# Attention steps with transposes first, scores second and weighing last, transposes three and weighing five units behind the scores

## The reference

```
x = x + LN(attention(LN(x)))
x = x + LN(feed_forward(LN(x)))

attention:  q = rms_norm(x wq), k = rms_norm(x wk), v = x wv      # 32 query heads, 8 key heads, 64 wide
            s = q k / 8 + alibi + mask      # token t sees tokens t-256 .. t
            out = softmax(s) v, then out wo
feed_forward: (silu(x gate) * (x up)) down, 1408 wide
```

## Time and profile before

| what | value |
|---|---|
| median of 3 runs | 1284.79 us (1283.95 to 1285.63) |
| the profiled execution | 1284.65 us, of which span 1282.9 us |
| PE busy | 1200.5 us (94%) |
| PEld busy | 1014.4 us (79%) |
| DVE busy | 910.8 us (71%) |
| ACT busy | 750.8 us (59%) |
| POOL busy | 386.0 us (30%) |

### The profile page before, as it was taken

The page is one execution under the profiler, slowest core; times in us unless marked ns, Lnnn a source line. Parts: engine busy times, 40 slices in busy tenths (PEclk is TensorE's granted clock), DMA queues, the critical chain, the costliest instruction groups (busy, mean ns, idle before and its releaser), DMA issues.

```text
span 1282.9 us, 29210 instructions
## 1 busy us (share of the span) xinstructions
PE 1200.5 (94%) x9016; PEld 1014.4 (79%) x9016; DVE 910.8 (71%) x2386; ACT 750.8 (59%) x1629; POOL 386.0 (30%) x460
## 2 busy tenths in 40 slices
PE   5999999997999899999999999999979979999998
PEld 4868778785777788888888898889867768888876
DVE  4597776867999788788888878788854355646364
ACT  3645455554999797777777777777732234232330
POOL 1000000001689675443445435443421100202021
PEclk9999999998999899999999999999989989999999
DMA  4216263455566565454555455454442252111110
GB/s 165 98 74 247 103 242 131 181 197 191 202 252 236 175 198 181 154 176 145 177 166 187 145 174 165 160 169 151 151 153 105 98 186 70 66 34 66 34 66 34
DMA packets 99259, 189.34 MB, mean 148 GB/s; under 512 B 8032, under 2 KB 36832, under 8 KB 99168
## 3 DMA queue, kind: packets, MB, share of 16 engines
q1 hardware_dynamic: 99168, 188.21, 43.1%
HBM read 116.54 MB, written 71.63 MB: 147 GB/s over the span
## 4 chain that ended last, share of the span: by engine, by line
PE 80%; DVE 9%; issue 4%; ACT 3%; DMA 3%; POOL 1%; DVEq 0%; SPq 0%; ACTq 0%; POOLq 0%
PE bank L1248 18%; PE bank L1379 17%; PE bank L1316 15%; PE bank L1270 10%; PE bank L1279 10%; PE bank L1297 2%; PE bank L1295 2%; PE bank L1296 2%; PE bank L1305 2%; DVE inv_rms L988 2%; DMA q_st<-q_scr 1%; DVE pT_lo L1041 1%; DVE oT_lo L1053 1%; DVE raw L967 1%; DMA w_stage<-wqT 1%
## 5 line engine op out<-in xcount | busy, mean ns | idle before, releaser
L826 ACT ACTIVATE p_sb<-u_sb,low 128x384 f32<-128x384 f32 (+2 forms) x512 | 274.4, 536 | 54.2 <-DVE low L1034 47.4
L1034 DVE CUSTOM_DVE_ANT_0 u_sb<-bank,bias 128x384 f32<-128x384 f32 (+2 forms) x512 | 231.3, 452 | 56.5 <-PE bank L1270 36.0
L1041 DVE TENSOR_TENSOR pT_lo<-bank,pT_hi 128x384 f16<-128x384 f32 (+2 forms) x512 | 232.3, 454 | 36.8 <-ACT pT_hi L833 21.4
L1270 PE MATMUL bank<-k_st,q_st 128*128 128x384 f32 (+2 forms) x1024 | 249.0, 325 | 7.3 <-DMA q_st<-q_scr 3.0
L833 ACT ACTIVATE pT_hi<-bank 128x384 f16<-128x384 f32 (+2 forms) x512 | 206.6, 403 | 68.5 <-PE bank L1279 64.8
L1279 PE MATMUL bank<-ident,p_sb 128*128 128x128 f32 x1152 | 219.0, 281 | 21.8 <-DVE pT_lo L1041 15.3
L1270 PEld LDWEIGHTS bank<-k_st,q_st 128*128 128x128 f32 x1024 | 176.5, 192 | 31.8 <-DVE v_out L1008 3.3
L1279 PEld LDWEIGHTS bank<-ident,p_sb 128*128 128x128 f32 x1152 | 137.9, 141 | 60.3 <-ACT p_sb L826 40.7
L583 POOL TENSOR_TENSOR rstd<-var_eps,minus_half 128x1 f32<-128x1 f32 (+1 forms) x31 | 23.4, 753 | 482.7 <-DVE var_eps L929 482.7
L1295 PE MATMUL bank<-v_st,pT_hi 128*128 128x65 f16 x1152 | 158.4, 193 | 0.5 <-DVE pT_lo L1041 0.5
L1296 PE MATMUL bank<-v_st,pT_hi 128*128 128x64 f16 x1152 | 158.7, 194 | 0.0
(11 more groups left out here) (115 smaller groups left out, 2324.2 us busy)
## 6 DMA issues: line engine op xcount, KB each, us to landing
q_scr<-qk SPq DMA_DIRECT2D x64, 512.0 KB, 2.7
q_st<-q_scr SPq DMA_DIRECT2D x32, 1024.0 KB, 7.8
k_st<-k_scr SPq DMA_DIRECT2D x64, 256.0 KB, 3.1
o_scr<-o_out SPq DMA_DIRECT2D x128, 128.0 KB, 2.5
o_in<-o_scr SPq DMA_DIRECT2D x16, 1024.0 KB, 5.1
k_scr<-qk SPq DMA_DIRECT2D x16, 512.0 KB, 3.1
z_in<-z_scr SPq DMA_DIRECT2D x8, 1024.0 KB, 5.9
v_scr<-v_out SPq DMA_DIRECT2D x4, 1040.0 KB, 5.9
```

Of the source, the lines that this page charges most:

```text
L826: nc.scalar.activation(p_sb[:, u % RING, 0:w], u_sb[:, u % RING, 0:w], ACT.Exp, scale=-1.0, bias=low[:, u % RING:u % RING + 1]).then_inc(p ...
L1034: nc.vector.tensor_tensor_reduce(out=u_sb[:, u % RING, 0:w], in0=bank[u % 2][:, 0:w], in1=bias[:, 2 * u // UNITS, u % REP, at:at + w], sca ...
L1041: nc.vector.tensor_tensor(pT_lo[:, u % RING, 0:w], bank[2 + u % 2][:, 0:w], pT_hi[:, u % RING, 0:w], ALU.subtract).then_inc(pT_ready, 1)
L1270: mm = nc.tensor.matmul(bank[u % 2][:, 0:w], q_st[:, s, r, P * i:P * i + P], k_st[:, s, part, P * key:P * key + w], start=(part == 0), sto ...
```

## The change

The order within a step and three lags change; no instruction is added, taken away or altered.

```diff
-LAGS = {"split": 3, "scores": 0, "transpose": 2, "exps": 0, "weigh": 4, "take": 5, "invert_sums": 6}
+LAGS = {"transpose": 3, "scores": 0, "split": 3, "exps": 0, "weigh": 5, "take": 6, "invert_sums": 7}
...
-            def unit_work(n, u):
+            def unit_work(n, u, kinds=("transpose", "scores", "weigh")):
                 for stage, nn, uu in due(n, u):
                     work = {"scores": scores, "transpose": transpose_p, "weigh": weigh_values}.get(stage)
-                    if work:
+                    if stage in kinds:
                         work(nn, uu)
 
             def attend(n, tile=None):
                 for u in range(UNITS):
-                    unit_work(n, u)
+                    unit_work(n, u, ("transpose",))
                     if tile is not None:
                         m, at = divmod(u - START, STEP)
                         if m in range(4) and at == 0:
                             transpose_o(tile, m)
+                    unit_work(n, u, ("scores",))
+                    if tile is not None:
                         m, at = divmod(u - START - 4, STEP)
                         if m in range(4):
...
                             project_o(tile, m, (2 * at, 2 * at + 1), bank[7])
+                    unit_work(n, u, ("weigh",))
```

## The result

The changed kernel takes 1304.66 us (median of 4 runs, 1302.59 to 1305.82) against 1284.82 for the kernel before (4 runs on the same chip): ratio 1.0155, 95% interval 1.0137 to 1.0172. It is slower, as I had forecast, but by 19.8 us and not by 4. The profiled execution took 1302.59 with a span of 1300.8.

The account below looks back on a forecast made before the run. PE was taken to bound projecting passes (1.50 us a step), a VectorE-ScalarE loop passes 0 to 4 (1.05). 13.5 + 5.1 - 4.7 + 0.5 - 10.3 = +4.1 on 1284.65 gave 1288.8, 8 in 10 within 1277 to 1297.

Parts of the forecast that it names:

- the loop: Passes 0 to 4: split, transposes, scores, `add_bias`, split takes 1.13 a step against 1.05; 2.7 a pass, +13.5 over five.
- the late scalings: Passes 0 to 2: rounding, `round_pT`, split and scaling become one chain; +1.5, +2.4 and +1.2, together +5.1.
- the wait for heads: Pass 3: PE's wait of 2.83 for the head loads goes, since slower passes let POOL catch up; -4.7.
- the drain: End of the attention passes: one more lag, +0.5.
- the projecting passes: Passes 5 to 15: PE's new order of neighbours exposes fewer weight loads; 0.94 saved a pass, -10.3 over 11.
- the anchor: Steps 0 to 11 of a projecting pass: step 12 starts at 13.97 against 14.1 before, so 0.1 saved.
- the neighbours in steps 12 to 31: Projecting passes: 0.055 saved a step in 15 of 20 steps, plus 0.09 of weighing moved out; 0.85 a pass.
- order worth nothing: Rival: weights are exposed as much elsewhere in the new order, passes 5 to 15 give 0; 1299, chance 0.05.

Follow-up runs that it names:

- E10: Changed kernel with TensorE's transposes turning among three banks instead of two in passes 0 to 4: 1300.0 us.
- E9: E1 with each head load issued one store of o earlier in SyncE's queue: 1305.0 us.
- E4: Changed kernel with VectorE's late scalings put between `add_bias` and the split: 1299.3 us.
- E12: Changed kernel with E4's and E9's edits and TensorE's old order in passes 0 to 4 and the first 12 steps of the others: 1281.7 us.
- E6: Changed kernel with one more, unread product per step on TensorE in passes 0 to 4: 1300.8 us, one run.
- E7: Changed kernel with GpSimd's late splits in passes 0 to 2 cut to 16 of 512 columns: 1301.1 us, one run.
- E1: Changed kernel with scores back at the head of TensorE's step, changed lags and VectorE order kept: 1309.0 us.
- E2: Changed kernel with all of TensorE's old step order, changed lags and VectorE order kept: 1301.1 us.
- E11: Changed kernel with the edits of E4, E9 and E10 together: 1283.8 us, ratio 1.0003.

## Why the prediction was wrong

**The sum.** I had +4.1 and the span grew by 17.9. Term by term, forecast and measured: the loop 13.5 and 13.0; the late scalings 5.1 and 10.5; the wait for heads -4.7 and -3.7; passes 5 to 14 -9.4 and -2.2; pass 15, the drain and the start -0.4 and +0.3. So two terms failed: the gain of the projecting passes came out 7.2 too small, and the late scalings cost 5.4 more.

**Direction and mechanism.** Slower, and through the loop that I named: right. E10 takes the loop away and E9 the order that makes it. In pass 4 the transposes' wait for `pT_lo` is 2.7 in the changed kernel, nothing in E10 and 0.6 in E9.

**The loop's price, 2.7 a pass.** Right in size: pass 4 grew by 2.6. The hops were off in detail in the two steps shown above. Scores behind transposes take 0.44 instead of 0.35, so scores to `add_bias` is 0.81 for my 0.73; and the split waits for its rounding, 0.61 for 0.47.

**The late scalings, +5.1 in passes 0 to 2.** This term was half of what it should have been. Passes 0 to 2 grew by 18.3, of which three loops are 7.8; 10.5 is left for a term of 5.1. Against loop and scaling as forecast (37.0, 37.9 and 36.7) 4.0 is missing in pass 0, 0.9 in pass 1 and 0.1 in pass 2. The chain itself was right: E4 gives back 5.4, and with the loop gone the scalings' place is worth 12.4 (E9 and E12). What I left out in pass 0 is that a slower loop also changes what runs beside what, and how much TensorE has to do: two scalings fell on GpSimd's splits and took 1.49 for 0.75, and the full clock came back 17.1 after the pass's start instead of 6.8. I took every duration from the kernel before, where the granted clock of passes 0 to 2 was 0.97 and no scaling of pass 0 was doubled. E6 puts the clock at about 2.4 in pass 0, and E7 the contention at 2.9, but some of that is clock too (0.75 to 0.82), each is one execution, and pass 0 varies by 1 to 2 without a cause in the program (E1, E2, E9). So the two don't add, and how they share the 4.0 is not settled.

The two loops are not terms of a sum either. E10 without the loop gives back 6.0 in passes 0 to 2, E4 with a shorter chain 5.4, E11 with both (and earlier loads) 16.5 of 116.6. Each holds the time up when the other is gone.

**The wait for heads in pass 3, -4.7.** Mostly right. The wait is 1.1 for 2.8 and pass 3 stands 1.4 above pass 4 for 5.1 before: -3.7. But the reason was only half there. I had seen that `pv_done` comes a step later, not that the store of o ahead of the load does too, and that the loads bind as soon as the loop is repaired.

**Projecting passes, -0.94 each.** They gained 0.22 each, so this term is 7.2 us short over passes 5 to 14. A slip in the count is small (0.8 and 0.09 are 0.89, not 0.85). Two steps of it failed. First, the anchor: I walked from the pass's first scores to the transposes of step 12 and called it the pass's start to start. Transposes at 636.68 are 13.95 into pass 8 (first scores at 622.73), just my 13.97; but the scores come 0.28 behind (636.96), and the kernel before has scores at the head of the step, so 0.28 was missing. From scores to scores steps 0 to 11 take 14.2 for 14.1 before: not 0.1 saved but 0.1 lost. Second, the neighbours in steps 12 to 31, where 0.85 was forecast and 0.4 came (27.2 to 26.8). Timeline of TensorE in pass 8, changed kernel (the weighing here has two tiles):

```profile
657.03 0.40 PE L1316 MATMUL bank<-wo_lo,oT_hi 128*128 128x512 f32 x1
657.26 0.40 PE L1316 MATMUL bank<-wo_hi,oT_hi 128*128 128x512 f32 x1
657.50 0.20 PE L1295 MATMUL bank<-v_st,pT_hi 128*128 128x65 f16 x1
657.54 0.20 PE L1296 MATMUL bank<-v_st,pT_hi 128*128 128x64 f16 x1
...
657.69 0.52 PE L1279 MATMUL bank<-ident,p_sb 128*128 128x128 f32 x3
657.97 0.60 PE L1270 MATMUL bank<-k_st,q_st 128*128 128x384 f32 x2
658.41 0.40 PE L1316 MATMUL bank<-wo_hi,oT_lo 128*128 128x512 f32 x1
```

The two products take 0.23 and 0.24: the 0.09 behind the weighing is gone, as I had it. Transposes and scores take 0.28 and 0.44, 0.72 for the 0.67 of the earlier trace rows; I had allowed 0.035 for that. And the first weighing product behind a long product takes 0.04 where one behind transposes takes 0.03, with 0.01 more ahead of it, for which I had nothing. A step gains about 0.02, not 0.055. So most of what the old order lost behind the weighing only moved to the scores behind the transposes and to the weighing behind the products. E2 has TensorE's neighbours in the old places under the new lags: its passes 6 to 14 take 41.1 each (370.3 for nine), 0.1 more than the changed kernel's. The order, which was the one gain of the change, is worth almost nothing here, though not quite: E12, with the new order from step 12 on, has 40.9.

That is close to what the rival *order worth nothing* (1299, chance 0.05) says. I had put it so low on the strength of one neighbourhood, a product behind transposes, which I had read as free. It wasn't: the product in the earlier trace rows takes 0.32 there, 0.09 more than behind another product. I had set the short time of the four transposes ahead of it (0.38, where 0.32/3 each makes 0.43) against that, and had put the 0.04 left over down to the transposes. The three-tile step has 0.05 in that place (0.72 for 0.67), and the weighing's 0.02 was in no row that I had.

The Trainium skill, "TensorE: Matmul & The Clock Gate", Part 3, The mechanism, as I used it, would have given no gain, and little came. But its reason isn't the one here: by it every load of all rows would be exposed alike, while the first product with `wo` takes 0.32 behind weighing and 0.23 behind scores above.

## What to carry to other kernels

When a reordering closes a new loop in a part where two engines are nearly full, price the loop, and then price again every duration in that part: what runs beside what changes, and so does the granted clock. Repair an experiment's next bottleneck before reading its time; E1 looked like the end of the right theory until its load waits were subtracted, and E9 showed it. Look for pairs of runs that are the same program in the part in question: E1 and E2 told how far passes 0 to 2 vary by themselves, and E9 and E12 what the scalings cost. And exposed weight loads are to be counted over the whole cycle of neighbours on TensorE, from one anchor to the same anchor.

## What the runs showed of the hardware

VectorE's `scalar_tensor_tensor` of 512 columns takes 0.745 alone and 1.49 when it starts 0.33 into a GpSimd `tensor_tensor` of 1.27 that reads the same memory; the GpSimd instruction keeps its 1.27. E1 and E6 show the same pair twice each (1.49 to 1.50, started 0.32 to 0.33 in). The Trainium skill, "SBUF — State Buffer", Who interferes with whom, says that a VectorE instruction with two inputs in SBUF contends with a GpSimd instruction that reads SBUF, and calls the ports that they share an exclusive lock. The direction agrees. The amount is smaller than a lock would give: blocked up to 322.63 and then 0.745 would end at 323.38, and the record ends at 323.18.

A product that is read by nobody went with a higher granted clock and with shorter passes: in E6 TensorE's granted clock in pass 0 was 0.91 for 0.75, and passes 0 to 2 took 113.9 for 116.6. That is one execution each, and the 2.7 are no more than the 3.1 by which E1 and E2 differ in these passes (110.3 and 113.4) with the same program there.
